# Macaron network with two sparse expert stages: b2 added one set ahead on GpSimd, fewer and wider register loads, two-set bodies on ScalarE

## What is computed

```python
x = x + 0.5 * _L0_ffn_ref(_layernorm(x), ...)   # mixture of experts, stage M0
x = x + _L0_attn_ref(_layernorm(x), ...)
x = x + 0.5 * _L0_ffn_ref(_layernorm(x), ...)   # mixture of experts, stage M1
x = x + 0.5 * _L1_ffn_ref(_layernorm(x), ...)
x = x + _L1_attn_ref(_layernorm(x), ...)
x = x + 0.5 * _L1_ffn_ref(_layernorm(x), ...)

# _moe, with D = 128, D_FF = 512, 8 experts, TOP_K = 2
logits = x_flat @ router_w
gate_vals, gate_idx = jax.lax.top_k(logits, TOP_K)
gate_w = jax.nn.softmax(gate_vals, axis=-1)
gates = jnp.zeros_like(logits).at[jnp.arange(N)[:, None], gate_idx].set(gate_w)
h = jax.nn.gelu(jnp.einsum('nd,edf->enf', x_flat, w1) + b1[:, None, :], approximate=False)
out = jnp.einsum('enf,efd->end', h, w2) + b2[:, None, :]
res = x_flat[None, :, :] + out
mu = jnp.mean(res, axis=-1, keepdims=True)
var = jnp.mean(jnp.square(res - mu), axis=-1, keepdims=True)
normed = (res - mu) * jax.lax.rsqrt(var + LN_EPS)
expert_out = normed * gamma[:, None, :] + beta[:, None, :]
y = jnp.einsum('end,ne->nd', expert_out, gates)
```

## Time and profile before

| | us |
|---|---|
| median of 3 runs | 3229.51 (3228.45 to 3241.72) |
| profiled execution | 3240.09 |
| its span, first to last instruction | 3238.0 |
| TensorE clock granted, mean over the span | 0.903 |
| busy PE, DVE, ACT, POOL | 2386.1, 2265.8, 1857.2, 1401.3 |
| first expert stage, from and to | 246 to 606 |
| second expert stage, from and to | 990 to 1356 |

### The profile page before, as it was taken

One profiled execution on the slowest core, in us unless ns is written; L12 is line 12 of the kernel. 1 busy time (PEld: TensorE's weight loads), 2 busy tenths in 40 slices (PEclk: granted clock), 3 DMA queues, 4 the chain that ended last, 5 costly groups with the idle time before them and its releaser, 6 DMA issues. The chain is left out here.

```text
span 3238.0 us, 66865 instructions
## 1 busy us (share of the span) xinstructions
PE 2386.1 (74%) x17707; PEld 1919.1 (59%) x17707; DVE 2265.8 (70%) x8247; ACT 1857.2 (57%) x4874; POOL 1401.3 (43%) x1366
## 2 busy tenths in 40 slices
PE   2217888384226787307868999999999999999587
PEld 2217676363225676305655877777777777778365
DVE  4325766685433666577977888888888888888697
ACT  2114444252213344235637988888888888889464
POOL 3553555302563555405532444444444444444365
PEclk9999999696558999758988999999999999999799
DMA  4133333312114333340000000000000000000000
GB/s 151 40 67 93 98 99 95 100 39 87 40 50 100 97 99 95 94 122 1 0 27 4 5 4 4 4 4 4 4 4 4 4 4 4 4 4 5 6 20 27
DMA packets 141736, 138.32 MB, mean 43 GB/s; under 512 B 17012, under 2 KB 127412, under 8 KB 140772
## 3 DMA queue, kind: packets, MB, share of 16 engines
q1 hardware_dynamic: 118932, 95.46, 9.8%
q0 software_dynamic: 17408, 35.82, 3.5%
q10 hardware_dynamic: 5200, 4.84, 0.5%
HBM read 59.31 MB, written 44.24 MB: 32 GB/s over the span
## 5 line engine op out<-in xcount | busy, mean ns | idle before, releaser
L2088 POOL TENSOR_TENSOR p_prob<-p_prob,p_inverse 128x512 f32<-128x512 f32 x512 | 533.3, 1042 | 797.0 <-DVE p_inverse L1912 797.0
L2005 ACT ACTIVATE p_prob<-p_neg,p_neg_max 128x256 f32<-128x256 f32 x1024 | 508.8, 503 | 40.2 <-DVE p_neg_max L1906 40.2
L1916 DVE SCALAR_TENSOR_TENSOR p_probT<-p_t_ps,p_probT 128x512 f16<-128x512 f32 x512 | 353.0, 689 | 195.1 <-ACT p_probT L2011 135.6
L883 ACT ACTIVATE p_e_hT<-p_e_h_ps,p_b 128x256 f32<-128x256 f32 x576 | 230.9, 474 | 352.9 <-PE p_e_h_ps L832 216.0
L997 POOL DMA_INDIRECT results_by_token<-p_e_result,p_e_slot x288 | 285.2, 990 | 309.6 <-DVE p_e_result L943 234.2
L706 POOL DMA_INDIRECT rows_by_expert<-p_r_z,p_r_target x256 | 249.4, 974 | 371.5 <-DVE p_r_z L561 258.2
L1906 DVE CUSTOM_DVE_ANT_0 p_neg<-p_s_ps,top_bias 128x256 f32<-128x256 f32 x1024 | 388.3, 416 | 0.8 <-ACT p_prob L2005 0.6
L2011 ACT ACTIVATE p_probT<-p_t_ps 128x512 f16<-128x512 f32 x512 | 304.9, 596 | 71.2 <-PE p_t_ps L2156 69.5
L841 PE MATMUL p_e_o_ps<-p_w,p_e_hT 128*128 x2304 | 308.2, 289 | 35.4 <-issue 22.7
L841 PEld LDWEIGHTS p_e_o_ps<-p_w,p_e_hT 128*128 128x128 f32 x2304 | 285.5, 201 | 55.9 <-issue 55.9
L2156 PE MATMUL p_t_ps<-top_ident,p_prob 128*128 128x128 f32 x2048 | 308.8, 273 | 7.0 <-POOL p_prob L2088 7.0
(11 more groups left out here) (266 smaller groups left out, 6157.3 us busy)
## 6 DMA issues: line engine op xcount, KB each, us to landing
p_e_affine<-p_affine SPq DMA_DIRECT2D x144, 192.0 KB
p_e_z<-rows_by_expert SPq DMA_DIRECT2D x144, 129.0 KB, 2.2
p_got<-results_by_token SPq DMA_DIRECT2D x64, 256.0 KB, 2.9
results_by_token<-p_e_result,p_e_slot POOLq DMA_INDIRECT x288
p_r_w<-in_w SPq DMA_DIRECT2D x2, 2048.0 KB, 7.6
p_w<-in_w SPq DMA_DIRECT2D x2, 2048.0 KB, 11.8
rows_by_expert<-p_r_z,p_r_target POOLq DMA_INDIRECT x256
p_reversed<-bias_by_distance ACTq DMA_DIRECT2D x2, 2048.0 KB, 17.1
```

Of the source, the lines that this page charges most:

```text
L1916: v.scalar_tensor_tensor(probT[k % 2][:, 1, :, :], t_ps[k % 2][:], PROB_SCALE, probT[k % 2][:, 0, :, :], ALU.mult, ALU.subtract).then_inc( ...
L2005: ins = act.activation(prob[k % PROBS][:, t, :], neg[k % 2][:, t, :], ACT.Exp, bias=neg_max[k % 2][:, t:t + 1], scale=-1.0, accum_out=tota ...
L2088: pool.tensor_tensor(prob[k % PROBS][:], prob[k % PROBS][:], inverse[k % PROBS][:].unsqueeze(2).to_broadcast([P, SEQ_TILES, SEQ]), ALU.mult)\
```

## The change

1. **GpSimd.** `take(n)` is cut in two. `add_b2(n+1)` now stands ahead of `give_back(n-2)`, `take_slots(n+1)` behind it. SP waits for the slot copy as well (`slot_ready`) before it loads new rows into the same buffer.
2. **Register loads.** One load instruction brings several values, without the check of bounds: two row starts or two experts on SP, four experts (two sets) on PE and ScalarE. `expert_of` is shifted by two entries. On PE the load stands between the first `up` and the first `turn` of every second set, no longer ahead of every `down`.
3. **ScalarE** runs its steps in bodies of two sets, not four.
4. **End of a stage on VectorE.** Roots and normalisation of set 34 come ahead of the residual of set 35, which gets roots of its own.
5. **Newton square.** `y * y` is written as scalar-tensor-tensor with a factor of 1.0.

```diff
@@ -96,3 +96,3 @@
-    chain.link(v.tensor_tensor(t, y, y, ALU.mult))
+    chain.link(v.scalar_tensor_tensor(t, y, 1.0, y, ALU.mult, ALU.mult))
     chain.link(v.scalar_tensor_tensor(t, t, -0.5, var, ALU.mult, ALU.mult))
@@ -396,2 +396,3 @@
 RING = 4
+EXPERTS_AHEAD = 2
@@ -414,3 +415,3 @@
             ("affine", [P, EXPERTS, 3, D], F32),
-            ("expert_of", [1, BLOCKS], I32),
+            ("expert_of", [1, EXPERTS_AHEAD + BLOCKS], I32),
             ("row_of", [1, BLOCKS], I32))}
@@ -596,3 +597,3 @@
                 chain.link(v.tensor_reduce(of_block[:, 0, :], reached[:], AX.X, ALU.add))
-                chain.link(v.tensor_scalar(w["expert_of"][:], of_block[:, 0, :], -1.0, float(EXPERTS - 1), ALU.add, ALU.min))
+                chain.link(v.tensor_scalar(w["expert_of"][:, EXPERTS_AHEAD:], of_block[:, 0, :], -1.0, float(EXPERTS - 1), ALU.add, ALU.min))
                 chain.link(v.tensor_tensor(reached[:], reached[:], rise[0:1, :].unsqueeze(1).to_broadcast([1, BLOCKS, EXPERTS + 1]),
@@ -758,5 +759,13 @@
-        def expert(eng, n, b):
+        def load_values(table, kind, highest):
-            return eng.value_load(w["expert_of"][0:1, bass.ds(n * SET + b, 1)], min_val=0, max_val=EXPERTS - 1)
+            _, values = nc.values_load_multi_w_load_instructions(
+                table, engines=[kind], min_val=0, max_val=highest,
+                skip_runtime_bounds_check_because="counted up from zero in whole blocks and clamped where the table is made")
+            return values
+        def experts(kind, n, sets):
+            first = n * SET + EXPERTS_AHEAD
+            return load_values(w["expert_of"][0:1, bass.ds(first, sets * SET)], kind, EXPERTS - 1)
@@ -773,5 +782,5 @@
             def load_rows(n, q):
-                for b in range(SET):
-                    at = sp.value_load(w["row_of"][0:1, bass.ds(n * SET + b, 1)], min_val=0,
-                                       max_val=EMPTY_START + EMPTY_BLOCKS * BLOCK_ROWS - BLOCK_ROWS)
+                starts = load_values(w["row_of"][0:1, bass.ds(n * SET, SET)], mybir.EngineType.SP,
+                                     EMPTY_START + EMPTY_BLOCKS * BLOCK_ROWS - BLOCK_ROWS)
+                for b, at in enumerate(starts):
                     sp.dma_start(z[q][:, tiles(b), :], dram_rows[bass.ds(at, BLOCK_ROWS), :].rearrange("(t p) d -> p t d", p=P))\
@@ -780,4 +789,3 @@
             def load_affine(n, q):
-                for b in range(SET):
-                    e = expert(sp, n, b)
+                for b, e in enumerate(experts(mybir.EngineType.SP, n, 1)):
                     sp.dma_start(affine[q][:, b, :, :], w["affine"][:, bass.ds(e, 1), :, :].rearrange("p e a d -> p (e a) d"))\
@@ -794,2 +802,4 @@
                             sp.sem_inc(carried, 1)
+                            sp.wait_ge(slot_ready, n)
+                            sp.sem_inc(carried, 1)
                         load_rows(n + 3, (q + 3) % RING)
@@ -846,24 +856,20 @@
-            def ring(j):
-                now = [expert(pe, j * RING, b) for b in range(SET)]
-                for q in range(RING):
-                    n = j * RING + q
-                    following = []
-                    for b in range(SET):
-                        if behind(j, q, 1):
-                            following.append(expert(pe, n + 1, b))
-                        down(n, q % 2, b, now[b])
-                        if behind(j, q, 1):
-                            up(n + 1, b, following[b])
-                        if behind(j, q, 2):
-                            turn(n + 2, b, *nth_in_ring(j, q, 2))
-                    now = following
             for b in range(SET):
                 turn(0, b, 0, 0)
+            now = experts(mybir.EngineType.PE, 0, 1)
+            pair = experts(mybir.EngineType.PE, 1, 2)
             for b in range(SET):
-                up(0, b, expert(pe, 0, b))
+                up(0, b, now[b])
                 turn(1, b, 0, 1)
-            for j in range(SETS // RING):
-                ring(j)
+            for n in range(SETS):
+                following, pair = pair[:SET], pair[SET:]
+                for b in range(SET):
+                    down(n, n % 2, b, now[b])
+                    if n + 1 < SETS:
+                        up(n + 1, b, following[b])
+                    if b == 0 and not pair and n + 2 < SETS:
+                        pair = experts(mybir.EngineType.PE, n + 2, min(2, SETS - n - 2))
+                    if n + 2 < SETS:
+                        turn(n + 2, b, (n + 2) // RING, (n + 2) % RING)
+                now = following
@@ -877,4 +883,3 @@
-            def hidden(n, b):
-                e = expert(act, n, b)
+            def hidden(n, b, e):
                 for half in range(HALVES):
@@ -886,11 +891,16 @@
-            def ring(j):
-                for q in range(RING):
-                    n = j * RING + q
+            def pair(j):
+                chosen = experts(mybir.EngineType.Activation, j * 2 + 1, 2 if there_is(j, 2) else 1)
+                for q in range(2):
+                    n = j * 2 + q
                     for b in range(SET):
-                        if behind(j, q, 1):
-                            hidden(n + 1, b)
-                        if behind(j, q, 2):
+                        if there_is(j, q + 1):
+                            hidden(n + 1, b, chosen[q * SET + b])
+                        if there_is(j, q + 2):
                             keep_high(n + 2, b)
+            def there_is(j, n):
+                return not isinstance(j, int) or 2 * j + n < SETS
             act.preload_act_table_set("gelu_and_others")
@@ -898,6 +908,9 @@
                 keep_high(0, b)
+            first = experts(mybir.EngineType.Activation, 0, 1)
             for b in range(SET):
-                hidden(0, b)
+                hidden(0, b, first[b])
                 keep_high(1, b)
-            set_rings(act, ring)
+            pair(0)
+            loop_groups(act, 1, SETS // 2 - 1, pair)
+            pair(SETS // 2 - 1)
@@ -926,5 +939,6 @@
-            def roots_of_pair():
-                chain.link(v.tensor_scalar(ln.var[:], ln.mv[:, :, 1], ln.eps, None, ALU.add))
-                rsqrt(v, chain, ln.rstd[:], ln.var[:], ln.tmp[:])
+            def roots(first, last):
+                at = slice(first * SET_TILES, last * SET_TILES)
+                chain.link(v.tensor_scalar(ln.var[:, at], ln.mv[:, at, 1], ln.eps, None, ALU.add))
+                rsqrt(v, chain, ln.rstd[:, at], ln.var[:, at], ln.tmp[:, at])
@@ -956,3 +970,3 @@
                         if q % 2 == 0:
-                            roots_of_pair()
+                            roots(0, 2)
                         normalise(n - 2, *nth_in_ring(j, q, -2))
@@ -965,5 +979,6 @@
             set_rings(v, ring)
-            residual(SETS - 1, RING - 1)
-            roots_of_pair()
+            roots(0, 1)
             normalise(SETS - 2, SETS // RING - 1, RING - 2)
+            residual(SETS - 1, RING - 1)
+            roots(1, 2)
             normalise(SETS - 1, SETS // RING - 1, RING - 1)
@@ -972,3 +987,3 @@
         def _(pool):
-            def take(n, nth, q):
+            def add_b2(n, nth, q):
@@ -976,6 +991,2 @@
                 pool.sem_inc(carried, 1)
-                if not early(n, RING):
-                    pool.wait_ge(returned[q % 2], (nth * (RING // 2) + q // 2 - 1) * SET_RETURNS)
-                    pool.sem_inc(carried, 1)
-                pool.tensor_copy(slot[q][:], z[q][:, :, D:ROW].bitcast(U32).rearrange("p t o -> p (t o)")).then_inc(slot_ready, 1)
                 pool.wait_ge(affine_loaded[q], nth * SET_LOADS + SET_LOADS)
@@ -990,2 +1001,8 @@
+            def take_slots(n, nth, q):
+                if not early(n, RING):
+                    pool.wait_ge(returned[q % 2], (nth * (RING // 2) + q // 2 - 1) * SET_RETURNS)
+                    pool.sem_inc(carried, 1)
+                pool.tensor_copy(slot[q][:], z[q][:, :, D:ROW].bitcast(U32).rearrange("p t o -> p (t o)")).then_inc(slot_ready, 1)
             def give_back(n, q):
@@ -1002,2 +1019,4 @@
                     n = j * RING + q
+                    if behind(j, q, 1):
+                        add_b2(n + 1, *nth_in_ring(j, q, 1))
                     if behind(j, q, -2):
@@ -1005,5 +1024,6 @@
                     if behind(j, q, 1):
-                        take(n + 1, *nth_in_ring(j, q, 1))
+                        take_slots(n + 1, *nth_in_ring(j, q, 1))
-            take(0, 0, 0)
+            add_b2(0, 0, 0)
+            take_slots(0, 0, 0)
             set_rings(pool, ring)
```

More of the change, by code:

```diff
@@ L965, in _ @@
             set_rings(v, ring)
+            roots(0, 1)
+            normalise(SETS - 2, SETS // RING - 1, RING - 2)
             residual(SETS - 1, RING - 1)
-            roots_of_pair()
-            normalise(SETS - 2, SETS // RING - 1, RING - 2)
+            roots(1, 2)
             normalise(SETS - 1, SETS // RING - 1, RING - 1)
```

## The result

The changed kernel takes **3140.6 us** (median of 4 runs, 3136.0 to 3146.1) against 3229.0 of the kernel before on the same chip: a ratio of 0.9718, 95% interval 0.9688 to 0.9749. That is -88 us, where -24 were forecast. Its profiled execution has a span of 3141.7 us against 3238.0, -96.3. Cut at the first transpose and the last scatter of either stage, the 96.3 us are: ahead of the first stage -3.5, first stage -23.6 (354.6 to 331.0), between them -1.8, second stage -29.4 (357.8 to 328.4), from there to the attention phase -0.6, the attention phase A1 **-37.8** (1268.7 to 1230.9, from the first to the last write of `p_probT` by VectorE), and +0.4 behind it. So four tenths of the gain are in a phase whose code the change does not touch: it holds not one instruction of the Newton iteration. The two stages together gave 53 us, where 24 were forecast.

A forecast was written before the change was run, and what follows sets the result against it. It took the bound to be a loop of hand-overs per pair of sets, held back while GpSimd issues scatters. From 3229.5 us, -8 for the stage ends and -16 for SP's loads, others 0, gave 3205 us, range 3150 to 3236.

The forecast's parts named there:

- The tails: End of each expert stage: GpSimd loses its idle time and the add between scatters, -4.0 us a stage, -8 together.
- SP's register loads: Fewer SP instructions per set send z and affine rows out 1 to 3 us earlier, shortening pairs: -16 us.
- the loop's 18.40 us: Time of one pair of sets in the expert stages where nothing is late, taken as the loop's bound.
- 18.2 us in 28 pairs: Excess of mean pairs over 18.40 us, bounding what earlier z rows can give; 20.8 us in all 32.
- The b2 add: GpSimd's add one set ahead: busy time unchanged, mid-stage residuals hardly wait for it, 0 in the loop.
- Four numbers per load: Loads of four on ScalarE and PE: 0.28 to 1.1 us per pair on ScalarE, covered by waiting; 0.
- Two-set bodies: ScalarE's loop takes twice as many turns; any cost lies in the same cover: 0, bounds 0 to +4 us.
- Newton square: On VectorE, tensor-tensor and scalar-tensor-tensor both take 166 ns on the same tile: 0.
- (a): Stage loop no longer tied to the scatters' end, as transposes reach ScalarE earlier: 17 us a pair, 3155 us; chance 0.10.
- (b): Held semaphores hide the z wait in long pairs too; only the stage ends gain: 3221 us; chance 0.18.
- (c): Late affine rows push GpSimd's add onto VectorE's roots, 1.7 us a pair, slower: 3255 us; chance 0.12.
- the z term: Gain in the stages from PE waiting less for z rows: -16 us, four fifths of 20.8.

The follow-up runs named there:

- after_less_tail: The changed kernel with the old order at the end of a stage on VectorE; 0.9766 of the kernel before, quick hand-over.
- loads_alone: The kernel before with only the wider register loads on SP, PE and ScalarE and the two-set bodies; 0.9879 of before, slow hand-over.
- act_alone: The kernel before with only the two-set bodies and wider loads on ScalarE; 1.0006 of before, quick hand-over.
- add_inside: The changed kernel with every second b2 add moved behind the first scatter of the next group; 0.9523 of the kernel before with quick hand-over, 0.9562 with slow.
- pad_half: The kernel before with 12 more VectorE instructions, one guess and Newton step behind each stage, result unused; 0.9892 of before, slow hand-over.

## Why the prediction was wrong

*The tails* (-8): right in kind, too large, and the new order is not what gives it. From the result of set 32 to the last scatter it took 25.1 us in either stage before. It takes 23.4 and 23.5 with the new order alone, 22.0 twice with the add moved alone, and 23.4 and 21.9 with the whole change: 5.1 us in both stages. With quick hand-over it takes 22.1 with the new order and 22.2 with the old one (`after_less_tail`): once the last residual no longer waits for its add, the order makes no difference. *But the step missed its largest effect*: "the extra roots of one set ... lie beside eight scatters of 10 us and cost nothing". They cost nothing there, and they move everything behind them on VectorE by 24 instructions, which is worth 38 us in another phase. The view that would have shown it was VectorE's waits of a phase that belongs to what is "touched by the change only through the Newton square": 58.5 us of waiting for issue in 13 times, in one place of a loop. I had read no waits behind the stages, so the program's position stood in no term of the sum, and nothing was given as the reason.

*SP's register loads* (-16): wrong in the mechanism, under in size. All loads together brought (18.98 - 17.82) x 16 + (19.12 - 18.01) x 16 = 36 us with slow hand-over. Late z rows are not what they cured: `loads_alone` still waits 28.2 us for them in 14 times, 3.9 less than before, with pairs that together are 36 us shorter; the versions with an unchanged loop have 32 to 40 us of these waits, the whole change 44.9. With quick hand-over SP's loads alone took them from 29.1 (`act_alone`) to 17.6 us, and the pairs stayed at 16.6. Neither was the loop's 18.40 us a floor: the trace of before itself has pairs of 17.9 and 17.6 us, and the shortest of the first stage is now 16.1. The bound "18.2 us in 28 pairs" rested on that floor, so the upper end of the term was wrong too. Nor was a wider load as cheap as one of the dropped ones: on SP, one with two experts takes 0.47 us in the median, where one with a single expert took 0.27. Which of the three loads counts with slow hand-over stays open: the single ones ran only on chips of the other kind, where none counts alone and SP's and PE's count equally behind the moved add.

*The b2 add* (0 in the loop): right where it was made, 0.9973 and no shorter pairs. On chips with quick hand-over it is worth 0.5 to 0.7 us a pair alone and opens the way for the loads.

*Four numbers per load* (0): right. The measured load of four takes 0.42 us on ScalarE in the median and 0.33 on PE, between my 0.28 and 1.1:

```profile
L762 PEldq TENSOR_LOAD <-p_expert_of x38: 328/332/718, 246.8 to 1255.5; - x38
...
L762 ACTq TENSOR_LOAD <-p_expert_of x38: 305/420/952, 248.0 to 1265.9; - x38
```

The Trainium skill's 200 ns for each register (Runtime: NRT & Kernel Launch, "Instruction fetch mechanics") would have been 0.8 us; the page speaks of loads from DRAM, and this table lies in SBUF. For this load on PE and ScalarE the trace decides against it (SP's step of 0.2 us from one value to two would fit). But that I put the dropped loads on PE at 0 was wrong at least behind the moved add (0.7 us a pair).

*Two-set bodies* (0): no cost showed, 1.0006 with ScalarE's loads, but only with quick hand-over, where the residual's wait for the add would also hide a small one; the *Newton square* (0) was not tried alone; the attention phase takes 1230.9 us in three versions without it, so it has no part in the 38 us.

*Rivals.* (a) had the right direction and a part of the size: the pairs came to 17.3 and 17.8 us where it said 17. Its mechanism did not come: in the first stage ScalarE still waits 59.2 us in 15 times for something remote (60.3 in 15 before). (b), only the tails, did not come either. (c) did not come, GpSimd's adds stand right behind the copies; but the price that it named, the add's hold on VectorE, is real and was already in the loop, and taking it away is what `add_inside` is paid for. No rival had the program's position.

Two figures of the prediction are off without weight: 20 us for 183 matmuls are 3.28 us a block of 30 and 13.1 a pair, not 3.31 and 13.2 (`add_inside` has a pair of 13.1 us), and a third of the z term gives 3215 us, not 3219.

## What to carry to other kernels

When a change adds or drops instructions on an engine, look at the turns of every loop that the engine runs later: an idle time for issue of the same few microseconds at each turn can come or go with the position alone, and a version with a dozen idle instructions more tells it in one run, and so does the count of instruction packets in the phase. Whether the stop costs anything depends on the engine: here VectorE's did and ScalarE's did not. Where several hand-overs of a loop are late together, single parts measure as nothing and the whole as much; test them upon the part that frees the first. Put a GpSimd elementwise operation beside VectorE work that it does not hold, and compare versions on more than one chip before calling a wait the bound.

## What the runs showed of the hardware

- VectorE's attention loop stands still for 2.9 us behind its branch (not ahead of it, as I had it when I sent `pad_half`) at all of its 13 turns back with the program of before, and at none with 12 or 24 instructions more ahead of it; the attention phase is 1268.7 or 1230.9 us. The stop comes with five packets of 8 KB on the instruction queue a turn, and goes with them. The Trainium skill (the same section of Runtime: NRT & Kernel Launch) says that a taken branch whose target is outside the two blocks of 256 instructions at hand forces a fetch before the engine goes on. The packets agree with it; which blocks are at hand, no run here shows.
- Chips differ. With slow hand-over, SP's register operation goes up to 0.72 us and ScalarE waits 60.3 us in 15 times for something remote in the first stage; on the other kind the same operation never exceeds 0.16 us, that wait is gone, and the same kernel is 4.8% faster (3091 to 3247 us). In the first stage before, 90 of 91 SP instructions of 0.6 us or more overlap a scatter or begin within 1 us behind one, of all SP instructions 51%. And the difference between the chips ends where the scatters end: `act_alone` reaches the attention phase 144.5 us earlier than the kernel before on the first chip, and from there on, without a scatter, the two take the same time (1268.6 and 1268.7 us for the phase). That scatters hold the hand-overs on such chips is still inferred from times, not shown by taking scatters away.

```profile
ACT p_e_hT L883 <- remote: 60.3, 15, 6.3
```

```profile
L761 SPq FUSED_REGOPS  x172: 46/152/159, 212.1 to 1176.1; - x172
```

- A b2 add of 1.18 us on GpSimd holds some VectorE operations for up to 2.0 us (0.17 to 0.35 otherwise), and the held one ends 0.02 to 0.16 us behind the add's end. Held were operations with all inputs in SBUF, with two tensors or with one; not held were those with one input in PSUM (the residual 0.68 us, the low part 0.42) and the statistics (0.88 us for four, 0.87 elsewhere).
